# A six-stage decoder kernel on one core: the third attention stage is prepared during the recurrence, and idle products run on the identity at the start of five stages

## The reference, cut to what matters

```python
x = x + mamba(norm(x))                       # L0_attn: a scan
x = x + cross_attention(norm(x), ctx)        # L0_xattn: stage "b"
x = x + attention_and_experts(norm(x))       # L0_ffn:   stages "c" and "d"
x = x + recurrence(norm(x))                  # L1_attn:  stage "r"
x = x + two_source_attention(norm(x), ctx)   # L1_xattn: stage "e"
x = x + experts(norm(x))                     # L1_ffn:   stage "f"
```

## Time and profile before

| | |
|---|---|
| median of 3 runs | 3362.09 us (3361.21 to 3363.53) |
| the profiled execution's own time | 3390.08 us |
| its span, first to last instruction | 3387.8 us |
| TensorE busy | 2774.7 us (82%), mean granted clock 0.926 |
| VectorE, ScalarE, GpSimd busy | 57%, 45%, 43% |
| stage b starts | 783.7 us |
| c | 1108.3 us |
| d | 1460.6 us |
| r | 2158.4 us |
| e | 2372.3 us |
| f | 3079.8 us |

### The profile page before, as it was taken

One profiled execution on the slowest core, in us unless ns is written; L12 is line 12 of the kernel. 1 busy time (PEld: TensorE's weight loads), 2 busy tenths in 40 slices (PEclk: granted clock), 3 DMA queues, 4 the chain that ended last, 5 costly groups with the idle time before them and its releaser, 6 DMA issues.

```text
span 3387.8 us, 49137 instructions
## 1 busy us (share of the span) xinstructions
PE 2774.7 (82%) x16644; PEld 1896.4 (56%) x16644; DVE 1931.8 (57%) x3400; ACT 1531.5 (45%) x2627; POOL 1459.2 (43%) x1508
## 2 busy tenths in 40 slices
PE   6878778865887688877999999699488888866998
PEld 2333323323555366633788885498355555545887
DVE  3788887783887488851122223401489888871111
ACT  4655555543776466520122221343366666641222
POOL 3666666663454477626000004400155556542444
PEclk8988989997999799988999999799799999977999
DMA  9600000000003000012566662100100011005775
GB/s 326 200 1 0 0 1 0 1 0 25 18 13 128 13 1 0 1 53 82 168 196 190 196 195 86 46 1 1 34 14 27 27 36 34 24 26 155 205 219 147
DMA packets 135983, 244.90 MB, mean 72 GB/s; under 512 B 16144, under 2 KB 107792, under 8 KB 125328
## 3 DMA queue, kind: packets, MB, share of 16 engines
q1 hardware_dynamic: 115344, 208.33, 19.0%
q0 software_dynamic: 20448, 34.11, 4.1%
HBM read 154.17 MB, written 90.05 MB: 72 GB/s over the span
## 4 chain that ended last, share of the span: by engine, by line
PE 34%; POOL 6%; issue 6%; DVE 6%; ACT 3%; another core or an unknown queue 1%; POOLq 1%; DMA 1%; SPq 0%; DVEq 0%; ACTq 0%
PE PS L2127 9%; PE PS L2085 5%; PE PS L1742 4%; PE PS L2372 4%; PE PS L2360 4%; POOL e_hs L1338 2%; PE PS L1193 1%; POOL rows_in_place L784 1%; POOL e_qs L1341 1%; DVE e_mx L1241 1%; PE PS L1138 1%; PE PS L1733 1%; POOL rows_by_expert L2016 1%; ACT e_pr L1305 1%
## 5 line engine op out<-in xcount | busy, mean ns | idle before, releaser
L506 POOL TENSOR_TENSOR u_in<-dtx,b_rep 128x512 f32<-128x512 f32 x256 | 339.0, 1345 | 210.5 <-ACT b_rep L487 198.4
L479 PE MATMUL PS<-scaled,ident 128*128 128x512 f32 x512 | 309.8, 690 | 71.9 <-DVE scaled L516 71.1
L522 DVE TENSOR_TENSOR_SCAN state<-PS,u_in 128x512 f32<-128x512 f32 x256 | 312.7, 1222 | 94.6 <-ACT PS L495 24.4
L2148 ACT ACTIVATE d_act_b<-PS 128x256 f32<-128x256 f32 (+1 forms) x188 | 78.7, 420 | 509.4 <-PE PS L2127 440.8
L2127 PE MATMUL PS<-d_unit_T,d_w 128*128 128x256 f32 x1248 | 284.0, 381 | 1.0 <-ACT d_unit_T L2137 1.0
L2160 DVE TENSOR_TENSOR d_hid<-d_act_b,PS 128x256 f32<-128x256 f32 (+1 forms) x188 | 87.4, 466 | 323.1 <-ACT d_act_b L2148 304.9
L495 ACT ACTIVATE PS<-dt,decay_rate 128x508 f32<-128x508 f32 x256 | 174.2, 685 | 186.7 <-DVE state L522 185.8
L1338 POOL TENSOR_TENSOR e_hs<-e_pr 128x512 f32<-128x512 f32 x128 | 162.9, 1273 | 221.6 <-ACT e_pr L1305 219.1
L2127 PEld LDWEIGHTS PS<-d_unit_T,d_w 128*128 128x128 f32 x1248 | 235.2, 191 | 32.0 <-issue 1.4
L2421 POOL DMA_INDIRECT out<-f_y,f_token x78 | 121.2, 1553 | 189.0 <-DVE f_token L2405 128.9
L2085 PE MATMUL PS<-d_w,d_hid 128*128 128x256 f32 x880 | 198.2, 380 | 1.5 <-DVE d_hid L2160 1.5
(11 more groups left out here) (424 smaller groups left out, 6386.7 us busy)
## 6 DMA issues: line engine op xcount, KB each, us to landing
d_w<-in_d_w SPq DMA_DIRECT2D x41, 1024.0 KB, 5.0
f_w<-in_f_w SPq DMA_DIRECT2D x39, 1024.0 KB, 5.0
rows_in_place<-blank SPq DMA_DIRECT2D x136, 272.0 KB, 4.2
d_w<-in_d_w SPq DMA_DIRECT2D x41, 512.0 KB
f_unit_rows<-rows_in_place SPq DMA_DIRECT2D x39, 272.0 KB, 4.9
rows_by_expert<-zeros SPq DMA_DIRECT2D x39, 256.0 KB, 2.8
d_unit_rows<-rows_by_expert SPq DMA_DIRECT2D x39, 256.0 KB, 4.0
out_by_expert<-d_y_rows SPq DMA_DIRECT2D x39, 256.0 KB, 4.1
```

The source lines that it names most:

```text
L479: nc.tensor.matmul(YB[:, c], ident[:], scaled[:, (KD * n + c) % RC], start=False, stop=n == NS - 1).then_inc(m_y, 1)
L506: nc.gpsimd.tensor_tensor(u_in[:, k % RU], dtx[:, p, c], b_rep[:, n % RB], ALU.mult).then_inc(m_u, 1)
L522: nc.vector.tensor_tensor_scan(state[:, k % 2], DECAY[:, k % RD], u_in[:, k % RU], 0.0, ALU.mult, ALU.add).then_inc(m_h, 1)
```

## The change

The diff has three parts.

1. Stage e is set up during stage r. `recurrence` is now built inside `attention("e", ..., ahead=...)`, so that the memory of e's weights and constants exists beside it. SP issues e's 18 loads and the first two context loads right after r's own; ScalarE, VectorE and GpSimd do e's setup after r's front, before the 128 steps. GpSimd, not VectorE, clears `rows`, `run`, `ones` and `va`. The turning back of `HS` and the additions to `X` leave r: groups 0 and 1 are done at the head of e, and groups 2 to 7 on TensorE after parts 1 to 6 of `front(0)`, with VectorE's additions after `early(1)`. They use PSUM banks 3 and 4; the constants' products use bank 5 (`SB`).
2. In all three attention stages `run` begins with `early(0)`; b and c do `setup_vector` on VectorE after `early(1)`, ScalarE waits for `parity` and `va` after `early(0)`, and TensorE waits for the loads only before the first query part.
3. `warm` issues products of the identity with itself, 512 columns wide, whose results nothing reads: 4 calls at the start of b, c and f, 3 at the start of d and r. Each product of 32-bit data is two instructions on TensorE.

```diff
+def warm(nc, bank, ident, times):
+    for _ in range(times):
+        nc.tensor.matmul(bank, ident[:], ident[:].unsqueeze(1).broadcast_to([128, 4, 128]), start=True, stop=True)
...
-        def setup_vector(dve):
-            nc.vector.memset(ones[:], 1.0)
+        def setup_pool(pool):
+            nc.gpsimd.memset(ones[:], 1.0)
             for e in range(E):
-                nc.vector.memset(run[:, e:e + 1], float(e * REGION // 128))
-            nc.vector.memset(rows[:], 0.0).then_inc(made, 1)
+                nc.gpsimd.memset(run[:, e:e + 1], float(e * REGION // 128))
+            nc.gpsimd.memset(rows[:], 0.0).then_inc(made, 1)
...
         def setup_vector(dve):
             dve.wait_ge(loaded, 16 * n_loads)
-            nc.vector.memset(PS[:, 6], 0.0)
             nc.vector.tensor_reduce(parity[:], ...).then_inc(parity_set, 1)
...
-            nc.vector.memset(va[:], 0.0).then_inc(ones_set, 1)
...
+            else:
+                nc.vector.memset(va[:], 0.0).then_inc(ones_set, 1)
+
+        def setup_pool(pool):
+            router["setup_pool"](pool)
+            nc.gpsimd.memset(va[:], 0.0).then_inc(ones_set, 1)
+
+        def constants_vector(dve):
+            nc.vector.memset(PS[:, 6], 0.0)
+            if table:
+                router["constants_vector"](dve)
+            if biased:
                 dve.wait_ge(x_done, 1)
-                nc.vector.tensor_tensor(v["bo"][:], v["bo"][:], FB[:, 0:D], ALU.add).then_inc(ready, 1)
+                nc.vector.tensor_tensor(v["bo"][:], v["bo"][:], SB[:, 0:D], ALU.add).then_inc(ready, 1)
...
         def early_vector(dve, g, p):
             yield stat_at
             after(dve, mean, g)
+            if ahead:
+                dve.wait_ge(h_added, 2 * g + 2)
...
+                    if is_first(g) and part == ("q", 0):
+                        pe.wait_ge(loaded, 16 * n_loads)
+                        if biased:
+                            pe.wait_ge(ready, READY_WIDE)
...
                 step.then_inc(full, 1)
+                if ahead and is_first(g) and 1 <= j < NG - 1:
+                    inner["add_tensor"](pe, j + 1, h_turned, h_added)
...
+            first()
             alone(early(eng, 0, 0))
+            second()
             alone(front(eng, 0, 0))
             alone(early(eng, 1, 1))
+            third()
...
         def tensor(pe):
-            pe.wait_ge(loaded, 16 * n_loads)
-            setup_tensor(pe)
-            run(pe, none, front_tensor, units_tensor, back_tensor, 0)
+            constants_tensor(pe)
+            if not ahead:
+                warm(nc, SB, ident, 4)
+            if ahead:
+                inner["add_tensor"](pe, 0, h_turned, h_added)
+                inner["add_tensor"](pe, 1, h_turned, h_added)
+            run(pe, none, front_tensor, units_tensor, back_tensor, 0, third=consts_taken)
...
         def scalar(act):
-            setup_scalar(act)
-            run(act, early_scalar, front_scalar, units_scalar, none, 2)
+            def after_setup():
+                act.wait_ge(parity_set, 1)
+                act.wait_ge(ones_set, 1)
+
+            run(act, early_scalar, front_scalar, units_scalar, none, 2, second=after_setup)
 
         def vector(dve):
-            setup_vector(dve)
-            run(dve, early_vector, none, units_vector, back_vector, 1)
+            def add(lo, hi):
+                for g in range(lo, hi if ahead else lo):
+                    inner["add_vector"](dve, g, h_turned, h_added)
+
+            def rest():
+                add(2, NG)
+                if not ahead:
+                    setup_vector(dve)
+                constants_vector(dve)
+
+            run(dve, early_vector, none, units_vector, back_vector, 1, first=lambda: add(0, 1), second=lambda: add(1, 2), third=rest)
...
-    def recurrence(tag, turn):
+    def recurrence(tag, turn, following):
...
+            sp.wait_ge(cleared, following["cleared"])
+            following["sync"](sp)
...
         def front_tensor(pe):
+            warm(nc, PS[:, 0], ident, 3)
...
-            pe.wait_ge(copied, 2 * TURNS + 1)
-            for b in range(B):
+        def add_tensor(pe, g, turned, added):
+            for b in range(GS * g, GS * g + GS):
                 if b % 2 == 0 and b >= 4:
                     pe.wait_ge(added, b // 2 - 1)
...
         def scalar(act):
             front_scalar(act)
+            act.wait_ge(cleared, following["cleared"])
+            following["scalar"](act)
...
             dve.sem_inc(tanhed[1], 1)
+            dve.wait_ge(cleared, following["cleared"])
+            following["vector"](dve)
...
         def pool(pl):
             front_pool(pl)
+            following["pool"](pl)
```

More of the change, by code:

```diff
@@ L609, in decoder_kernel, with early_router @@
     mamba_mem.end()
-    def early_router(tag, mem, table, FB, number, full, empty, x_in, plan):
+    def early_router(tag, mem, table, FB, SB, number, full, empty, x_in, plan):
         t = lambda name, shape, dtype=F32: mem.take(f"{tag}_{name}", shape, dtype)
@@ L867, in attention @@
         bv_wide = t("bv_wide", [128, KD, 128]) if biased else None
+        cT = t("cT", [128, 2, KD, GT]) if "ctx" in sets else None
+        va = t("va", [128, 2, A, GS, NH, 2 * DH])
+        st, mvs, rs = t("st", [128, GS, 6]), t("mvs", [128, GS, 2]), t("rs", [128, 8, GS])
+        spare, spare2 = t("spare", [128, 1]), t("spare2", [128, 1])
+        full, empty, back_in = s("full"), s("empty"), s("back_in")
+        FB = PS[:, 7]
+        SB = PS[:, 5]
+        router = early_router("f", mem, table, FB, SB, lambda *x: fb_number[x], full, empty, back_in, ROUTE) if table else None
+        inner = ahead() if ahead else None
         xn = None if rms else t("xn", [128, 2, GS, D])
@@ L901, in attention @@
         kept, inverted = s("kept"), s("inverted")
[L902 to L905, removed]
+        scored, shifted, maxed, exped, turned, taken, valued, mixed, recip, joined, x_done = map(s, (
+            "scored", "shifted", "maxed", "exped", "turned", "taken", "valued", "mixed", "recip", "joined", "x_done"))
         x1_in, x1_mean, x1_scale = s("x1_in"), s("x1_mean"), s("x1_scale")
-        router = early_router("f", mem, table, FB, lambda *x: fb_number[x], full, empty, back_in, ROUTE) if table else None
+        h_turned, h_added = (s("h_turned"), s("h_added")) if ahead else (None, None)
         n_loads = len(wide) + len(vecs) + (len(router["v"]) if table else 0)
@@ L1419, in attention, with nothing, run @@
         s_x1c = s("x1c")
-        def run(eng, early, front, units, back, n=None):
+        def nothing():
+            return
+        def run(eng, early, front, units, back, n=None, first=nothing, second=nothing, third=nothing):
             def turn(g, p):
@@ L1641, in recurrence @@
         ring = t("ring", [128, KD, 2 * WIN, B])
+        apart = t("apart", [128, 1024])
         HS = t("HS", [128, KD, B, L])
-        loaded, bias_set, vec, mean, chain, scaled_by, normed, copied, turned, added = map(s, (
-            "loaded", "bias_set", "vec", "mean", "chain", "scaled_by", "normed", "copied", "turned", "added"))
+        loaded, bias_set, vec, mean, chain, scaled_by, normed, copied = map(s, (
+            "loaded", "bias_set", "vec", "mean", "chain", "scaled_by", "normed", "copied"))
         in_T, taken = ([s(f"{n}{c}") for c in range(KD)] for n in ("in_T", "taken"))
@@ L1758, in tensor, with add_vector @@
                 for c in range(KD):
-                    step = nc.tensor.transpose(PS[:, 4 + b // 2 % 2, (b % 2 * KD + c) * 128:(b % 2 * KD + c) * 128 + 128], HS[:, c, b], ident[:])
+                    step = nc.tensor.transpose(PS[:, 3 + b // 2 % 2, (b % 2 * KD + c) * 128:(b % 2 * KD + c) * 128 + 128], HS[:, c, b], ident[:])
                 if b % 2:
                     step.then_inc(turned, 1)
+        def add_vector(dve, g, turned, added):
+            x_seq = X.rearrange("p g s d -> p (g s) d")
+            for b in range(GS * g, GS * g + GS, 2):
+                dve.wait_ge(turned, b // 2 + 1)
+                nc.vector.tensor_tensor(x_seq[:, b:b + 2], x_seq[:, b:b + 2],
+                                        PS[:, 3 + b // 2 % 2].rearrange("p (b d) -> p b d", b=2), ALU.add).then_inc(added, 1)
         def scalar(act):
             front_scalar(act)
+            act.wait_ge(cleared, following["cleared"])
+            following["scalar"](act)
             act.wait_ge(copied, 1)
@@ L2363, in tensor @@
         def tensor(pe):
+            warm(nc, PS[:, 3], ident, 4)
             turn_rows(pe, 0)
@@ L2438, in decoder_kernel @@
     h_mem.end()
-    recur = recurrence("r", 0)
     f_mem = Stage(nc, ())
@@ L2449, in decoder_kernel @@
                  expert_i=f("expert_i", [128, UNITS], I32), start_i=f("start_i", [128, UNITS], I32))
-    e_attn = attention("e", 1, ["x", "ctx"], out_w=True, table=table, result=out)
+    after_recurrence = {"cleared": 4}
```

(3 more changed lines are left out.)

62 lines of the change are left out of this document (27 added, 35 removed).

## The result

The changed kernel takes 3305.51 us (median of 4 runs, 3303.68 to 3308.04) beside 3361.65 for the kernel before (4 runs): 56.1 us less, ratio 0.9834 with a 95% interval of 0.9817 to 0.9851. On another chip it took 3336.23 beside 3390.43, 54.2 less, ratio 0.9838 (0.9824 to 0.9851). The forecast was 3313.6, from 3303 to 3324, a gain of 48.5.

What follows compares the result with a forecast made beforehand. TensorE is on 34% of the last-ending chain; the change touches only stage seams, taken as paid in full. Savings of 30.3 + 7.7 + 9.0 + 1.5 = 48.5 us from the median gave 3313.6 us, range 3303 to 3324.

Steps and rivals of the forecast that it cites:

- The bound: At stage seams: no engine enters a stage before the others, so what is saved there is saved at the end.
- Part 1, ahead of the front: Seam between r and e: with e prepared during r, `front(0)` starts 36.8 us earlier.
- passing the stage: From r's last `HS` copy into e: 0.80 us, as VectorE idled before its first instruction in r.
- Part 1, the additions in the front: Front of e: turning and adding groups 2 to 7 there costs 6.5 us, leaving 30.3 saved.
- The rival that priced this at 11.8: Front of e: engines wait at each bank or clock stays low, 48 transposes cost 11.8 us; total 3319; chance 0.13.
- What r takes in: Stage r: e's loads, constants, setup and memsets fit into idle time there, costed at 0.
- Memset in the way of r's copies (rival): Stage r: GpSimd's memset holds VectorE's last two `xT` copies, first step 8 us late; total 3322; chance 0.08.
- The rival of late loads: Stage r: e's loads land late and delay the first Tanh; landing at 2246 gives 3369 us; chance 0.02.
- Part 2: Starts of b and c: the new order brings the first `xT` copy 7.7 us earlier in b, 9.0 in c.
- Part 3: Idle products at stage starts: 1.5 us saved, from -2.5 to +7, with 1.5 in f and 0 elsewhere.
- The rival, clock held up everywhere: All five starts: idle products hold TensorE's clock up, saving 6.6 us in place of 1.5; total 3308.5; chance 0.12.

Runs made afterwards that it cites:

- p5: Changed kernel with e's loads and whole setup back at the head of e, GpSimd still clearing `va`: 3350.60 us, ratio 0.9883.
- p6: Changed kernel with all of `HS` turned and added at the head of e, none in the front: 3343.78 us, ratio 0.9864.
- p8: Changed kernel with `va` cleared five times on GpSimd during r: 3341.98 us.
- p7: Changed kernel with `va` cleared in b and c right after `early(0)`, ahead of the wait for the loads: 3332.73 us, ratio 0.9826.
- p2: Changed kernel without any of the five sets of idle products: 3338.27 us, ratio 0.9850.
- p3: Kernel before the change, with the idle products alone added: 3388.70 us beside 3390.43, ratio 0.9995.
- p9: Changed kernel with `va` cleared early in b and c, idle products none in d and r, 9 calls in c, 5 in e: 3293.19 us, ratio 0.9807.
- p10: Changed kernel with idle products none in d and r, 9 calls in c, 5 in e, without early clearing of `va`: 3304.31 us, ratio 0.9830.
- p11: Changed kernel with idle products in f alone: 3308.10 us, ratio 0.9843.

## Why the prediction was right, and where it was off

- **The bound.** "What is saved at a seam is saved at the end" held: what b, c and e gain up to their first maxima is what their stages get shorter by, within 1 or 2 us.
- **Part 1, ahead of the front.** 36.8 forecast, 37.8 measured. The term that was most off is passing the stage, 0.64 of the 1.0: 0.80 was read where all waited for GpSimd; here the last to come is VectorE, and it took 0.16. p5 and p6 show the two halves, loads with scalings and additions, each at its price (24.8 us against 24 to 26, 19.2 against 19.4).
- **Part 1, the additions in the front.** 6.5 forecast. The first execution of the kernel before took 24.7 from first transposes to first maximum, a second 26.0, the changed one 29.5 and 29.0: 3 to 5. I took 1.10 for eight transposes, a duration with its pipeline's end in it; between two matrix products they displace 0.88, and 5.3 in all. A rise of the clock during the first query products (3.04 in place of the 3.69 that the four took before) gave back some more. The rival that priced this at 11.8 is excluded. Of the rows, the first two are of before (its first transposes stand at 2407.10), the third of after:

```profile
2410.67 3.69 PE L1138 MATMUL PS<-e_xT,e_wq 128*128 128x512 f32 x4 [0.69 <-ACT e_xT L1093]
...
2431.82 1.23 DVE L1241 TENSOR_REDUCE e_mx<-PS 128x8 f32<-128x1024 f32 x1 [26.55 <-PE PS L1184]
```
```profile
2323.67 3.04 PE L1153 MATMUL PS<-e_xT,e_wq 128*128 128x512 f32 x4
```

- **What r takes in.** Costed at 0, and it is: r's first Tanh comes 32.6 us after its first DMA (33.0 before), its last `HS` copy 201.0 (201.7). The cover was thinner than I wrote. GpSimd's memset (6.93) held VectorE's scalings, so that they ended at 2142.7, 9 us before the first `HS` copy. The price when that cover is gone is p8's 8 to 9 us. The rival of late loads fell: the first Tanh did not move.
- **Memset in the way of r's copies (rival).** Wrong for `xT`: the memset began before the last of them (2134.75), and that took 1.02. Copies from PSUM were not held in p8 either. The 1008 ns of the earlier trace rows were of the kind that is, and ended 0.09 after a GpSimd instruction did. The memset, in the changed kernel:

```profile
2133.24 6.93 POOL L1007 MEMSET e_va<- 128x8192 f32 x1
```

  The Trainium skill, "SBUF — State Buffer", "Who interferes with whom", names copies and scalings among what can contend and describes a lock for one instruction; p8 agrees, with the memsets' ends at the ends of VectorE's waits.
- **Part 2.** b 7.7, measured 6.6 in one pair of profiles and 8.9 in the other, because `va` waits for the loads: VectorE works out `parity`, for which it needs them, 5.7 after the first issue in one and 4.3 in the other. c 9.0, measured 9.3 at the first `xT`; the rest of c's 10.6 I can't place, each part being within 1 us. p7 shows that the memset was the gate. No run takes the new order in b and c out by itself; its gain is read from the stages.
- **Part 3.** 1.5 forecast, measured 2.0 (p2) and 1.7 (p3), neither clear of nothing by its interval; the places show f as where it comes from (1.3 to 3.1) and d as a small cost (0.2 to 0.5). The rival, clock held up everywhere, fell for this kernel: the clock had fallen again before b's and c's query products. (The rival's sum in the prediction has a slip: 2 and 2 in b and c, 2.6 in f and 1 in d are 7.6, not 6.6, and give 3307.5.) Windows of the changed kernel:

```profile
787.00:793.00 6.00, 1.76 (x7) 0.61 (x5) 4.12 (x3) 1.77 (x4) 1.60 (x4) 1.00 0.41 146
794.00:800.00 6.00, 5.37 (x7) 2.27 (x8) 0.00 (x0) 1.18 (x2) 0.00 (x0) 0.50 0.00 0
1099.40:1103.00 3.60, 3.60 (x8) 1.43 (x8) 3.25 (x13) 0.00 (x0) 1.36 (x3) 1.00 0.59 195
1108.00:1117.00 9.00, 5.89 (x13) 3.02 (x14) 3.09 (x2) 1.37 (x2) 7.97 (x15) 0.50 0.01 2
```

  But the mechanism is real where the products reach the work: p9 and p10 bring it to c and e, for some 3 us each at the first maximum (p10 beside p11). The gap left behind the products made the difference here: in b of the changed kernel TensorE idled 4.17 us before its second four transposes, and the query products ran at 0.50; in p7 it idled 0.77 there, and they ran at 1.00. The Trainium skill's rule that activity releases a throttled clock ("TensorE: Matmul & The Clock Gate", Part 1) agrees with both.

The sum was short by 5 to 8 of 54 to 56 us: some 1 ahead of e's front, 2 or 3 in the additions, 1.6 in c, 1 in f, and 1 in b and r together. The first three lie outside what two executions differ by, b and f do not. All the misses went the same way, so the number itself owes something to the width of the range: 3305.5 lies under the 3307 to 3317 that I gave the forecast by itself, and nearer to the rival of the held-up clock (3308.5 as I wrote it), whose mechanism the runs exclude. What held is the mechanism, seam by seam.

## What to carry to other kernels

At a seam list what each engine does between the old stage's last instruction and the new one's first product, and move whatever needs no result of the old stage (loads, constants, memsets) into the stretch where the engine that does it idles; then look again, since the next gate (here the memset of `va` in b and c, 3.5 us in p7 and 11.1 between p10 and p9) stands right behind. Idle products pay only if they run up to the work that counts; put ahead of a gap they are lost, and put ahead of ready work they delay it. A price taken from a row's duration is too high for pipelined instructions: take it from start to start.

## What the runs showed of the hardware that I had not expected

- A GpSimd memset of 8192 columns (6.9 us) holds VectorE's scalings and its copies within on-chip memory until it ends: 3.5 and 7.0 us for operations that take 0.17, and 7.1 for each of two copies into `HS`, where two together take 0.67 otherwise. Two-operand products, reductions and copies from PSUM went on beside it.
- One stage of the same program took 668 to 670 us on some chips and 695 to 703 on others, by waits whose releaser the profile doesn't show; a difference of two profiles from different chips says nothing without a comparison stage by stage.
